# Media cross-attention and feed-forward loops laid out afresh: values as the stationary operand, p scaled before its transpose on DVE

## What is computed

```
q = layernorm(x) @ Wq * 64**-0.5                 # 256 -> 1024 = 16 heads x 64
k, v = split(media @ Wkv)                        # 128 -> 2 x 1024
sim = q k^T per head, with masked media positions at -inf
attn = softmax(sim);  out = attn @ v             # per head
x = x + tanh(attn_gate) * (out @ Wo)             # 1024 -> 256
x = x + tanh(ff_gate) * (gelu(layernorm(x) @ W1) @ W2)   # 256 -> 1024 -> 256
```

## Time and profile before

| | us |
|---|---|
| runs of the kernel | 1684.55, 1692.62, 1694.56 (median 1692.62) |
| the profiled execution's own time | 1686.46 |
| its span, first to last instruction | 1684.4 |
| PE busy in the span | 1552.4 (92%) |
| PEld busy | 1339.0 (79%) |
| DVE busy | 967.5 (57%) |
| ACT busy | 668.8 (40%) |
| POOL busy | 246.7 (15%) |

### The profile page before, as it was taken

How to read it: one execution, slowest core, us unless ns; L and a number is a source line. 1 busy time by engine, 2 the same in 40 slices (tenths; PEclk the granted TensorE clock), 3 DMA queues, 4 the chain that set the end, 5 groups by cost and what they waited for, 6 DMA issues and landing times.

```text
span 1684.4 us, 31094 instructions
## 1 busy us (share of the span) xinstructions
PE 1552.4 (92%) x11106; PEld 1339.0 (79%) x11106; DVE 967.5 (57%) x2163; ACT 668.8 (40%) x1773; POOL 246.7 (15%) x346
## 2 busy tenths in 40 slices
PE   5879899899899899999889999998999999899899
PEld 4747677667667679999778878887988878788799
DVE  2646655646646675676274646564655555647554
ACT  1314334434424462222454444443336353535332
POOL 0134324324324300000000000000100000000010
PEclk9989999999999889999999999999999999999999
DMA  3203000000000020000100000002000000000000
GB/s 144 69 13 107 4 1 3 3 0 3 3 0 1 1 82 1 0 0 1 53 5 4 3 3 3 1 1 82 0 33 25 4 3 3 3 0 1 1 25 26
DMA packets 13224, 30.20 MB, mean 18 GB/s; under 512 B 2400, under 2 KB 8800, under 8 KB 12512
## 3 DMA queue, kind: packets, MB, share of 16 engines
q1 hardware_dynamic: 13152, 29.23, 4.9%
HBM read 27.13 MB, written 2.10 MB: 17 GB/s over the span
## 4 chain that ended last, share of the span: by engine, by line
PE 77%; DVE 10%; issue 6%; ACT 3%; POOL 2%; DMA 0%; DVEq 0%; SPq 0%; ACTq 0%; POOLq 0%
PE bank L774 69%; PE bank L787 8%; DVE nmax L1258 2%; DVE pT L1157 2%; DVE stats L1187 1%; ACT p L1472 1%; DVE xn L1233 1%; POOL kbd L1652 1%; DVE xn L1237 1%; POOL rstd L1619 1%; DVE o_rounded L1342 0%; ACT hT L1423 0%; DVE aggr L1192 0%; DVE xn L1235 0%; DMA p<-in_media 0%
## 5 line engine op out<-in xcount | busy, mean ns | idle before, releaser
L1472 ACT ACTIVATE p<-bank,nmax 128x128 f32<-128x128 f32 x1024 | 285.4, 375 | 394.3 <-DVE nmax L1258 393.9
L774 PE MATMUL bank<-v,pT 128*128 128x65 f32 (+2 forms) x2048 | 258.1, 263 | 46.1 <-issue 25.0
L774 PEld LDWEIGHTS bank<-v,pT 128*128 128x128 f32 x2048 | 252.3, 194 | 54.0 <-issue 42.3
L1258 DVE TENSOR_REDUCE nmax<-bank 128x4 f32<-128x512 f32 x256 | 170.1, 686 | 161.7 <-PE bank L774 161.4
L774 PE MATMUL bank<-w_ff_rounded,hT_rounded 128*128 128x256 f32 x944 | 218.4, 287 | 0.8 <-DVE kbd L1320 0.8
L774 PE MATMUL bank<-kbd,hT 64*128 64x128 f32 (+1 forms) x1280 | 205.1, 342 | 5.0 <-ACT hT L1423 3.9
L787 PEld LDWEIGHTS bank<-consts,p 128*128 128x128 f32 x1040 | 125.4, 143 | 100.4 <-issue 79.5
L774 PE MATMUL bank<-xT_rounded,w_ff_rounded 128*128 128x256 f32 x864 | 196.8, 286 | 4.5 <-issue 3.0
L1157 DVE COPY pT<-bank 128x512 f32<-128x512 f32 x256 | 174.6, 682 | 34.8 <-PE bank L787 34.3
L774 PE MATMUL bank<-xn_rounded,w_ff_rounded 128*128 128x256 f32 x608 | 172.9, 284 | 0.0
L787 PE MATMUL bank<-consts,p 128*128 128x128 f32 x1040 | 161.6, 278 | 7.5 <-ACT p L1432 5.0
(11 more groups left out here) (147 smaller groups left out, 2798.8 us busy)
## 6 DMA issues: line engine op xcount, KB each, us to landing
ctxT<-in_ctxT SPq DMA_DIRECT2D x32, 128.0 KB, 2.4
w_ff<-in_w1b SPq DMA_DIRECT2D x6, 640.0 KB, 6.6
w_att<-in_w2a SPq DMA_DIRECT2D x1, 3072.0 KB, 10.6
w_att<-in_w3a SPq DMA_DIRECT2D x1, 3072.0 KB, 10.3
w_att<-in_w1a SPq DMA_DIRECT2D x1, 2432.0 KB, 12.3
hT<-in_xT SPq DMA_DIRECT2D x8, 256.0 KB, 3.1
o<-in_x SPq DMA_DIRECT2D x8, 256.0 KB, 3.1
w_ff<-in_w2b SPq DMA_DIRECT2D x1, 2048.0 KB, 7.4
```

The lines of the kernel that those rows point to most:

```text
L774: return pe.matmul(dst, lhsT, rhs, start=first, stop=last)
L1258: dve.tensor_reduce(nmax[:, ph.place[s] % P_RING, :], bank[:, :].rearrange("p (h t) -> p h t", h=QUAD), AX_X, ALU.max, negate=True).then_i ...
L1472: t = act.activation(p_ring[i % P_RING][:, part], bank[:, part], ACT.Exp, bias=nmax[:, i % P_RING, j:j + 1])
```

## The change

- **Values.** The four `values` steps of a sequence go. `oT2` now makes the transposed output directly: for each head, v (128x64) is stationary and pT (128 columns) moves, and the result goes to partitions 0 to 63 (even heads, from one `pT_ring` buffer) or 64 to 127 (odd heads, from the other) of one bank. v loses its column of ones. The four transposes of `o` go.
- **1/sum.** ACT's exponential also gives the sum of its row (`accum_out`), and a new step `share` on DVE takes the reciprocals of a pair of groups and multiplies both p tiles (128x512) by them in place, before the transpose.
- **p buffers** for media are eight instead of four.
- **Order.** The media loop's body has eight equal slots (`media_slots`), one per pair of groups, and the pipeline runs on across iterations: scores of pair k, share of k-1, transposes of k-3, oT2 of k-4. Side steps (projections, norm, `wo`) are dealt to the slots by `media_sides`.
- **wo and w2** are made per sequence, each into 256 columns of a bank, and x is added to per sequence (`half`, `end`).
- **nT2's low part** is a step of its own.
- **Feed-forward body.** Starts with `w2` of unit A; the hidden layers of both units are made ahead for the next iteration.
- **Banks** in phases 3 to 6: in 3 and 5 four for scores and four for the rest, in 4 and 6 four for `w2` and four for the rest.
- **Between phases**: steps of the next phase are dealt into the slots of the last iteration; Wq's low part lies in `kbd`; the step `zero` (POOL) goes.

```diff
+MEDIA_RING = 8
+def media_slots():
+    pairs = [("media", u, b, 2 * i) for u in range(UNITS) for b in range(ROWS) for i in range(GROUPS // 2)]
+    n = len(pairs)
...
+    for k in range(n // 2, n // 2 + n):
+        new, turned, done, shared = (pairs[i % n] for i in (k, k - 3, k - 4, k - 1))
+        out = done[1:3] + (done[3] // 2,)
+        slots.append((of(k - 4, ("oT2",) + out)
+                      + of(k - 3, *[("turn",) + turned[:3] + (turned[3] + i,) for i in range(2)])
+                      + of(k - 4, ("oT2_low",) + out),
+                      of(k, *[("scores",) + new[:3] + (new[3] + i,) for i in range(2)])
+                      + of(k - 1, ("share",) + shared)))
+def media_sides():
+    def part(u):
+        other = B_ if u == A_ else A_
+        values = (here if u == A_ else ahead)(*[("v2", other, j // 2, j % 2) for j in range(IC // 2)])
+        keys, queries = (ahead(*[(k, u, j) for j in range(IC // 2)]) for k in ("k2", "q2"))
+        return [(values[:1], ahead(("norm_q", u)) + keys[:3] + ahead(("scale_q", u))),
+                (values[1:2], ahead(("nT2", u)) + here(("wo", u, 0), ("half", u))),
+                (ahead(("nT2_low", u)) + values[2:3], ahead(("mrow", u)) + keys[3:] + queries[:2]),
+                (values[3:], queries[2:] + here(("wo", u, 1), ("end", u)))]
+    return part(A_) + part(B_)
+def media_body():
+    return [first + early + second + late for (first, second), (early, late) in zip(media_slots(), media_sides())]
```

The feed-forward body, and the banks:

```diff
 def steps_ff2(norms, pre):
+    (out_a, half_a, rest_a), (out_b, half_b, rest_b) = (
+        (here(("w2", u, 0)), here(("half", u)), here(("w2", u, 1), ("end", u))) for u in range(UNITS))
+    early = ahead(*norms[0::2]) + out_a + ahead(*norms[1::2]) + half_a
+    if ("w1", A_, 0) in pre:
+        turns, lows = (ahead(*[(k, u) for u in range(UNITS)]) for k in ("nT2", "nT2_low"))
+        return (early + rest_a + turns + out_b + lows + half_b + ahead(*hidden2(A_)) + rest_b + ahead(*hidden2(B_)))
...
+        if index in (3, 5):
+            of_scores = [s for s in jobs if s[0] == "scores"]
+            others = [s for s in jobs if s[0] != "scores"]
+            self.bank = {s: i % QUAD for i, s in enumerate(of_scores)} | {s: QUAD + i % QUAD for i, s in enumerate(others)}
```

The engines' side:

```diff
+            # TensorE
             def oT2(ph, it, s, bank):
                 u, b, j = s[1:]
-                pe.wait_ge(*after(ph, it, ("values", "media", u, b, 2 * j + 1), "normed"))
-                turn(s, ph.bank[s], [o[u][:, b * INNER + m * P:b * INNER + (m + 1) * P] for m in range(4 * j, 4 * j + 4)])
+                pe.wait_ge(*after(ph, it, ("turn", "media", u, b, 2 * j + 1), "copied"))
+                pe.wait_ge(*after(ph, it, ("v2", u, b, j), "copied"))
+                for i in range(QUAD):
+                    for side in range(2):
+                        to = bank[side * HD2:(side + 1) * HD2, i * P:(i + 1) * P]
+                        t = mm(to, v_view("media", u)[:, b, j * 8 + 2 * i + side, :], pT_ring[side][:, i * P:(i + 1) * P], True, True)
+                t.then_inc(sems[s[0], "mm"], 1)
+            # VectorE
+            def share(ph, it, s, bank):
+                u, b, g = s[2:]
+                i = ph.place[("scores",) + s[1:]] % P_RING
+                dve.wait_ge(*after(ph, it, ("scores", "media", u, b, g + 1), "exp"))
+                dve.reciprocal(rshare[:, i:i + 2, :], rsum[:, i:i + 2, :]).then_inc(sems[s[0], "rinv"], 1)
+                dve.wait_ge(*after(ph, it, s, "rinv"))
+                for n in range(2):
+                    p = p_of(ph, s[:4] + (s[4] + n,)).rearrange("q (h t) -> q h t", h=QUAD)
+                    t = dve.tensor_tensor(p, p, rshare[:, i + n, :].unsqueeze(2).broadcast_to([P, QUAD, P]), ALU.mult)
+                t.then_inc(sems[s[0], "done"], 1)
+            # ScalarE, in scores
+                    if s[1] == "media":
+                        t = act.activation(p[:, part], bank[:, part], ACT.Exp, bias=nmax[:, i, j:j + 1],
+                                           accum_out=rsum[:, i, j:j + 1])
```

More of the change, by code:

```diff
@@ L124, in attention @@
         slot = []
-        if i < len(groups) and groups[i][0] != "media":
+        if i < len(groups):
             slot += here(("scores",) + groups[i])
-        elif i < len(groups) and i % 2 == 0:
-            slot += here(("scores",) + groups[i], ("scores",) + groups[i + 1])
         if 0 <= i - SKEW_T < len(groups):
@@ L230, in steps_mlp1 @@
                  (here(("end", A_), ("end", B_)), 2 * h, 2 * h + 1),
[L231 to L233 removed]
+                 (ahead(*norms[3:]), 2 * h, 2 * h),
+                 (ahead(*pre[:cut]), 2 * h, 2 * h),
+                 (ahead(*pre[cut:]), 2 * h + 1, 2 * h + 1))
 def steps_attn2(norms, pre):
[L237 to L238 removed]
@@ L240, in steps_attn2 @@
[L240 to L256, removed]
@@ L259, in steps_ff2 @@
-def steps_ff2(norms, pre):
[L260 to L268, removed]
+    slots = media_body()
+    if ("scores", "media", A_, 0, 0) in pre:
+        return [s for slot in slots for s in slot]
@@ new lines, in steps_attn2 @@
+    of_this = [[s for s in slot if not s[1]] for slot in slots]
+    n = len(of_this)
+    norm_a, scale_a, norm_b, scale_b = ahead(*norms)
+    (turn_a, low_a, *hidden_a), (turn_b, low_b, *hidden_b) = (ahead(*pre[u * len(pre) // 2:(u + 1) * len(pre) // 2]) for u in range(UNITS))
+    for at, more in ((1, [norm_a, norm_b]), (2, [scale_a, scale_b]), (4, [turn_a, turn_b]),
+                     (5, [low_a, low_b] + hidden_a[:2]), (6, hidden_a[2:3])):
+        of_this[at] = of_this[at] + more
+    of_this[-1] = of_this[-1][:-2] + hidden_a[3:] + of_this[-1][-2:] + hidden_b
@@ new lines, in steps_attn2 @@
+    return [s for slot in of_this for s in slot]
+def steps_ff2(norms, pre):
+    (out_a, half_a, rest_a), (out_b, half_b, rest_b) = (
[4 more added lines that the diff above has]
+        return (early + rest_a + turns + out_b + lows + half_b + ahead(*hidden2(A_)) + rest_b + ahead(*hidden2(B_)))
+    first, second = (pre.index(("q2", u, 0)) if pre else 0 for u in range(UNITS))
+    third = (first + second) // 2
+    return (early + ahead(*pre[:first]) + rest_a + ahead(*pre[first:third]) + out_b + half_b + ahead(*pre[third:second])
+            + rest_b + ahead(*pre[second:]))
@@ L346, in count, with emptied @@
         return it * self.of_kind[kind] + (before + self.place[step] + 1)
+    def emptied(self, step):
+        if step[0] in ("wo", "w2") and step[2] == 0:
+            step = ("half", step[1])
+        elif step[0] in LAST:
+            step = ("end", step[1])
+        return step, EMPTIED[step[0]]
     def earlier(self, step, n):
@@ L906, in turn_p @@
             def turn_p(ph, it, s, bank):
-                pe.wait_ge(*after(ph, it, ("scores",) + s[1:], "exp"))
-                turn(s, ph.bank[s], [p_ring[ph.place[s] % P_RING][:, j * P:(j + 1) * P] for j in range(QUAD)])
+                if s[1] == "media":
+                    pe.wait_ge(*after(ph, it, ("share",) + s[1:4] + (s[4] // 2 * 2,), "done"))
+                else:
+                    pe.wait_ge(*after(ph, it, ("scores",) + s[1:], "exp"))
+                turn(s, ph.bank[s], [p_of(ph, s)[:, j * P:(j + 1) * P] for j in range(QUAD)])
             def values(ph, it, s, bank):
```

159 lines of the change are left out of this document (83 added, 76 removed), and 2 rows, old and new, of the table EVENTS.

## The result

The changed kernel takes 1593.3 us (median; 1592.4 to 1594.2) against 1693.6 for the one before, measured with it. The ratio is 0.941, 95% interval 0.937 to 0.946: some 100 us faster. I had stated 1580, and 1545 to 1622. The profiled execution took 1592.67 us with a span of 1590.9, 94 us less than the profiled one before (1686.46), so traces compare 94 us and medians 100.

What follows compares the result with a forecast made beforehand. PE was taken to bound the kernel. Six steady iterations save 68 us and the joints 24 + 16 = 40, together 108: 1578 from the profiled 1686.5, 1584 by the median, stated as 1580, range 1545 to 1622.

Steps and rivals of the forecast that it cites:

- The bound: Media iteration: PE is the engine to count, at its start-to-start rates; 79.6 us falls to 68.2.
- Even slots: Media loop: nothing waits within a slot, so the 8.0 us of pipeline fill and drain an iteration go.
- The oT2 job: Media values, 16 records a job: column halves overlap as the score job's row halves do, 1.1 us.
- the rival: In oT2 the column halves don't overlap: 1.95 us a job, about 1615 us in total; chance 0.23.
- DVE in the first slots: First slot of each half: PE waits for DVE's k2 copies and oT2's low part, 1.9 us, twice an iteration 3.8.
- ACT hidden: Media iteration: exponentials with a sum take ACT from 35.4 to 41 us, hidden under PE.
- The feed-forward: Feed-forward iterations: same products and transposes as before, steady at 23.9 us.
- The joints: Between phases: of 56 us of idle and lost clock, 24 are won, bounds 0 and 40.
- the two others: Two iterations' worth of media work outside the six steady ones: they gain (17.0 - 8.8) x 2 = 16 us.
- Slots no shorter: Rival, media loop: DVE's in-order work and waits fill each slot to 9.7 us, nothing is measured; chance 0.05.
- slower: Rival, oT2 job: each column-half record runs by itself, iteration 92.8 us, total about 1775; chance 0.05.
- signs of being wrong: oT2 jobs 1.7 us or more; media iterations 64 or above 72; PE waiting for share; joints idling 10 us each.

Runs made afterwards that it cites:

- the halves apart: The changed kernel with oT2's eight matmuls reordered, the four of the lower column half first, then the four of the upper: 1615.0 us.
- POOL's version: The changed kernel with share's two multiplications on POOL, the reciprocal still on DVE: 1575.5 us.
- the one without products: The changed kernel without share's multiplications, the reciprocals kept, so the division by the sum is left out: 1578.0 us.
- without the sums: The changed kernel whose exponentials don't give their sums, rsum set to 1 once, DVE still multiplying: 1590.8 us.

## Why the prediction was right, point by point

- **The bound.** PE at its rates: right. The iteration was to be 68.2 us and is 67.9. By slots, the four of a half take 6.91, 8.99, 8.04 and 10.06 us where the rates gave 6.7, 7.4, 7.85 and 9.85. Three slots are some 0.2 us over their PE work; one waits. (The hit is a little better than its parts: an iteration's oT2 jobs came out 0.6 us cheaper and its waits 0.6 shorter than walked, and the quiet slots together some 0.7 longer than with the 1.0 that I gave to hand-overs.)
- **Even slots.** I put the whole 8.0 us between work and length down to fill and drain. Some 1.4 of them were lost clock. It went too, so the sum came out. The prediction expected a clock of 1.00 in the loops, but had no term for what that is worth and no reason why it should come.
- **The oT2 job.** I took 1.1 by the score job's row and kept 1.95 as the rival. It is 1.03, and the experiment with the halves apart shows that alternation takes 0.48 us off: pairs of records start together. Without alternation the job is 1.51 and not 1.95, since four records still overlap there. The rule of the Trainium skill ("TensorE: Matmul & The Clock Gate", Part 3) that weight loads overlap matmuls in flight only in another row group was read as 1.95; the trace disagrees with that reading. The column tiles' measured speed-up on the same page of the Trainium skill pointed the right way.
- **DVE in the first slots.** Named before the run, with its instruction: the k2 copy, then oT2's low part. Walked as 1.1 and 0.5 us of waiting, shown as 0.81 and 0.18; the slot loses 1.6 us where I walked 1.9, 3.2 an iteration instead of 3.8. POOL's version gives back 1.9 of them and the one without products 1.6; the rest stays in the same slot, 8.0 us with POOL where the rates gave 7.4. What the walk didn't tell is that reordering wouldn't cure it: once the wait moved whole to the next job that needed DVE, once about half of it did.
- **ACT hidden.** Right in the loop (67.98 without the sums, too), wrong in the joints to a media phase, where the sums cost 1.4 us of idle each, and up to 2.7 and 2.4 with the clock.
- **The feed-forward.** Right: 24.1 against 23.9.
- **The joints: the term that was mis-sized.** "I take 24 of these 56" us of idle and lost clock. Idle went from 41.8 to 37.1, and the stretches times one less the clock give 12 instead of 14: about 7 of 56. It is not that nothing was won. Four joints gave 16 us of idle and clock together, and the joint to block 3 took back 10: 7 more of idle, and a clock of 0.92 where it was 0.97. The longest wait there, 3.92 us for the addition of `half` that the new order puts behind norm and scale on DVE, has no counterpart before, and the experiment that moves `half` ahead takes about half of it away. PE also waits there 2.57 and 2.31 us for ACT, behind the exponentials of the prologue's score jobs (0.7 less each without the sums), and 3.4 us for k2 copies on DVE, which I didn't test. From the mark in the last MLP iteration (784.28 and 780.75) to the end it is 900.1 against 810.2 us: 90 less, of which 70 are steady iterations, 16 the cheaper PE work in the two others by my count, and some 4 all else. The forecast's 108 less the 17 to 20 that the joints fell short is what was measured. Another 3.5 us came before that mark, where nothing was changed, and that is luck, as are 6 of the 100 us between the medians: the profiled executions are 94 apart.
- **How the gain divides.** An iteration's 11.7 us: PE has 8.8 less to do (17.0 less 8 x 1.03). If the old order had turned two thirds of that into time, as it did with 6.2, cheaper work alone is an estimated 6 us, the even slots a little over 6, the clock 1.4, and DVE's multiplication takes back 1.9. Neither part was run alone in full, and which of them keeps the clock up is open.
- **Small slips.** 1.72 and 0.25 are 1.97, where I went on with 1.95. "Slots no shorter" and "slower" have 0.05 each among the rivals and 0.04 each in the line on directions. Neither touches the forecast. Of the signs of being wrong, one came in one place: the joint to block 3 still idles for over 10 us.

## What to carry to other kernels

Count PE's work by the distance between starts, not by busy time, and hold the remainder up against the order: here 71.6 of 79.6 us, and even slots brought the loop within 5 us of its count (67.9 against 62.8 with oT2 as measured). Take the lost clock out of that remainder first; here it was 1.4 of the 8. Then walk each slot for the in-order engine that feeds the banks; an average load of 70% (48 of 68 us) still cost 2 us an iteration, because its work came in the two shortest slots, and giving 10 us of it to an engine that stood idle helped, though that takes half as long again, where moving it within DVE helped half as much at best. Don't book the joints between loops as won because the list of steps has been filled: look at each joint by itself, for a step that now stands behind another on an in-order engine and holds a bank.

## What was not expected of the hardware

- Sixteen records of float32 matmuls on one column half after another take 1.51 us, though 8 x 0.86/4 = 1.72 is what the columns cost in a projection, because four records of the two halves overlap. Alternating halves takes 1.03.
- A float32 record that moves 65 columns cost as much as one that moves 128: 0.84/8 = 0.105 us in the old values, against 0.109 in the changed kernel with the halves apart, where nothing runs beside it. So swapping the operands, 128 columns past 64 stationary ones, won nothing a record. The gain is that two records run side by side, and the 0.45 us of transposing `o` that goes with each job.
- The untouched phases 0 to 2 took between 779 and 795 us to the same mark in different executions, with the granted clock of their middle between 0.97 and 0.93. Between kernels that differ by 5 us, the distance from a mark to the end told more than the total.
